# The last phase of an attention and mixture-of-experts kernel: half groups over seven PSUM banks, root scratch in the eighth, two additions on VectorE

## The chip, the cores and the metric

One core of a Trainium2 chip runs the whole program. The metric is the device time of one execution in microseconds (us); lower is better. The engines are named as in the profile: PE is TensorE's matmul side and PEld its weight loads, DVE is VectorE, ACT is ScalarE, POOL is GpSimd, SP is SyncE, whose queue issues most DMAs.

## The reference

A block of attention and a block of experts, each between layer norms, over 16 x 256 = 4096 tokens of width 256:

```
x = x + layernorm(attention(layernorm(x)))          # 16 heads of 128, weights = codes * scales
h = layernorm(x)
scores = softmax(h @ gate.T); keep 3 of 8 groups of experts, then 6 of 64 experts
slot of a token in an expert: its position, cut at 95 (CAPACITY 96: all later ones share slot 95)
out[e]  = (silu(buf[e] @ Wg[e].T) * (buf[e] @ Wu[e].T)) @ Wd[e].T
y       = sum over the 6 experts of weight * out[slot]
shared  = silu(h @ Sg.T) * (h @ Su.T) @ Sd.T
x = x + layernorm(y + shared)
```

The last line is what the change is about. All tokens past a capacity of 95 in an expert get the same output row, that of slot 95, weighted by their own weights.

## The kernel before

The program runs in three stages. Attention goes over 8 blocks of 512 tokens, then the 64 experts run one after the other (with the shared expert of the last blocks slipped between), and then comes the last phase, from about 1314 us to the end. Everything in it goes by groups of 512 tokens: NP = 8 groups, each held as 4 tiles of 128 tokens x 256. Every engine has its own instruction stream in program order, and waits on semaphores that others count up; nothing is scheduled at run time.

What the last phase does for a group g:

- SP loads two partial sums, `Y[0]` and `Y[1]`, from DRAM into `fin[g][:, 0]` and `fin[g][:, 1]` (two DMAs of 512 KB a group, 16 in all, semaphore `fl`). The experts have added their rows there; for groups 0 to 5 `Y[0]` also holds the shared expert's part. For groups 6 and 7 (`g >= LATE`) the shared part stays in SBUF, in `YL[g]`.
- POOL adds the two halves of `fin` (`last_sum`, L960, two instructions of 128x512 a group, semaphore `fa`).
- PE builds the sum in PSUM: `last_over` multiplies the transposed weights of the tokens past capacity, `W95T` (64 partitions), with the 64 rows `OUT95` (L1198); for groups 6 and 7 it adds `YL` by a matmul with the identity (L1203); `last_add` adds the sum from `fin` by a matmul with the identity (L1209, semaphore `fp`). One fp32 matmul stands in the profile as two instructions. `LB_` gives each group a pair of PSUM banks, four pairs in turn, so group g+4 must wait until ACT has read group g (semaphore `fn`).
- DVE takes mean and variance out of PSUM (`last_stats`: L1474 and L1478), and finds one over the square root for a batch of groups by a magic constant and three Newton steps: twelve small instructions on 128x8 or 128x4 numbers in SBUF, each of which waits for the one before (L1481 to L1487, the helper `step`; semaphore `fs`). `BATCH` says which groups share such a root: (0, 1), (2, 3), (4, 5), (6), (7).
- ACT normalizes from PSUM into `fin[g][:, 0]` with these scales and biases (L1355, four instructions a group).
- The residual `x1[g]` is added, the first half of the group by POOL (L970, semaphore `fx`) and the second by DVE (L1495, `fy`), and SP stores the group.

`POOL_LAST` is POOL's order: "s0 s1 s2 s3 x0 s4 x1 s5 x2 x3 s6 s7 x4 x5 x6 x7", with s for a sum and x for a residual. DVE does the statistics and root of a batch, and then the residuals of the batch before it. PE does the overs of groups 0 to 3, then the additions, and from group 4 on each over just ahead of its addition.

Of the kernel before, what the change touches and what calls it, by code (L numbers as in the profile page):

```python
# [18 lines left out]
E = 64  # L19
# [7 lines left out]
BATCH = ((0, 1), (2, 3), (4, 5), (6,), (7,))  # L27
POOL_LAST = "s0 s1 s2 s3 x0 s4 x1 s5 x2 x3 s6 s7 x4 x5 x6 x7"
EPS = 1e-5
# [5 lines left out]
LATE = 6  # L35
# [148 lines left out]
def build(nc, x, wc, wsc, wo_c, wo_s, bqkv, bo, gateT, sguT, sdT, ewT, ewd, out):  # L184
    ctx = ExitStack()
    with ctx:
# [36 lines left out]
        ident = sb("ident", [128, 128])  # L223
# [87 lines left out]
        def flat(a, dims):  # L311
# [20 lines left out]
                 "lf lc xr fo hd bi yi dd lb sw swh swl sg ssl saf sah sal sdn sy et ebt eg esl eac eo eow wix wt wtc fa fp fd fs fn fx fy").split()  # L332
# [455 lines left out]
        def _(eng):  # L788
# [99 lines left out]
            for g in range(NP):  # L888
# [3 lines left out]
            for g in range(NP):  # L892
                eng.wait_ge(s["fx"], g + 1)
                eng.wait_ge(s["fy"], g + 1)
                eng.dma_start(out[g * 512:(g + 1) * 512, :].rearrange("(t p) d -> p t d", p=128), fin[g][:, 0, :, :]
                              ).then_inc(s["fo"], 16)
# [4 lines left out]
        def _(eng):  # L901
# [54 lines left out]
            def last_sum(g):  # L956
                f = fin[g]
                eng.wait_ge(s_fl[g], 32)
                for h in range(2):
                    r = eng.tensor_tensor(half(f[:, 0], h), half(f[:, 0], h), half(f[:, 1], h), ALU.add)  # L960
                r.then_inc(s["fa"], 1)

            def last_x1(g):
                f = fin[g]
                eng.wait_ge(s["fn"], 2 * g + 1)
# [4 lines left out]
                eng.tensor_tensor(half(f[:, 0], 0), half(f[:, 0], 0), half(x1[g], 0), ALU.add).then_inc(s["fx"], 1)  # L970

            for name in POOL_LAST.split():
                (last_sum if name[0] == "s" else last_x1)(int(name[1:]))
# [3 lines left out]
        def _(eng):  # L977
# [212 lines left out]
            eng.wait_ge(s["wtc"], NP)  # L1190
            for k in range(4):
                eng.wait_ge(s_o95[k], 16 * E // 4)

            def last_over(g):
                if g >= 4:
                    eng.wait_ge(s["fn"], 2 * (g - 4) + 2)
                for t in range(4):
                    eng.matmul(LB_[g % 4][t // 2][:, t % 2 * 256:(t % 2 + 1) * 256],  # L1198
                               W95T[:, (4 * g + t) * 128:(4 * g + t + 1) * 128], OUT95[0:E, :],
                               start=(t % 2 == 0), stop=False, skip_group_check=True)  # L1200
                if g >= LATE:
                    for t in range(4):
                        eng.matmul(LB_[g % 4][t // 2][:, t % 2 * 256:(t % 2 + 1) * 256], ident[:, :],  # L1203
                                   YL[g][:, t, :], start=False, stop=False, skip_group_check=True)

            def last_add(g):
                eng.wait_ge(s["fa"], g + 1)
                for t in range(4):
                    r = eng.matmul(LB_[g % 4][t // 2][:, t % 2 * 256:(t % 2 + 1) * 256], ident[:, :],  # L1209
                                   fin[g][:, 0, t, :], start=False, stop=(t % 2 == 1), skip_group_check=True)  # L1210
                r.then_inc(s["fp"], 1)

            for g in range(4):
                last_over(g)
            for g in range(NP):
                if g >= 4:
                    last_over(g)
                last_add(g)
# [3 lines left out]
        def _(eng):  # L1222
# [127 lines left out]
            for g in range(NP):  # L1350
                eng.wait_ge(s["fs"], batch_of(g) + 1)
                for h in range(2):
                    for t in (2 * h, 2 * h + 1):
                        c = 4 * g + t
                        r = eng.activation(fin[g][:, 0, t, :], LB_[g % 4][h][:, t % 2 * 256:(t % 2 + 1) * 256],  # L1355
                                           ACT.Identity, bias=fNW[:, 3, c:c + 1], scale=fNW[:, 1, c:c + 1])
                    r.then_inc(s["fn"], 1)
# [3 lines left out]
        def _(eng):  # L1361
# [108 lines left out]
            def last_stats(gs):  # L1470
                for g in gs:
                    eng.wait_ge(s["fp"], g + 1)
                    for t in range(4):
                        r = eng.bn_stats(fST[g][:, t, :], LB_[g % 4][t // 2][:, t % 2 * 256:(t % 2 + 1) * 256])  # L1474
                step(r)
                c0, c1 = 4 * gs[0], 4 * gs[-1] + 4
# [10 lines left out]
                eng.scalar_tensor_tensor(out=b, in0=fMV[:, c0:c1, 0], scalar=-1.0, in1=y, op0=ALU.mult, op1=ALU.mult  # L1487
                                         ).then_inc(s["fs"], 1)

            def last_x1(g):  # L1490
                f = fin[g]
                eng.wait_ge(s["fn"], 2 * g + 2)
                if g < 4:
                    eng.wait_ge(s["xr"], 64)
                eng.tensor_tensor(half(f[:, 0], 1), half(f[:, 0], 1), half(x1[g], 1), ALU.add).then_inc(s["fy"], 1)  # L1495

            for n, gs in enumerate(BATCH):
                last_stats(gs)
                if n:
                    for g in BATCH[n - 1]:  # L1500
                        last_x1(g)
            for g in BATCH[-1]:
                last_x1(g)
# [35 lines left out]
```

## Time and profile before

| | us |
|---|---|
| median of 3 runs | 1377.25 (1375.5 to 1378.28) |
| the profiled execution | 1383.52 |
| its span in the trace | 1381.8 |
| last phase: first over to DVE's last instruction | 1316.6 to 1375.7 |
| PE busy over the span | 1223.8 (89%) |
| DVE, ACT, POOL busy over the span | 869.4, 826.4, 922.2 |

The profiled execution lies 1.7 us above its own span and 6.3 us above the median of the runs. Shares over the span say nothing of the last phase, which is a twentieth of it and has other limits than the rest.

### The profile page before, as it was taken

The page shows a single profiled execution, that of the slowest core. Times are in us where ns is not written, and L with a number is a line of the kernel's source. Part 1 is how long each engine was busy: PE and PEld are TensorE (multiplying, and loading weights), DVE is VectorE, ACT ScalarE, POOL GpSimd, SP SyncE. Part 2 cuts the span into 40 slices and gives each one's busy share as a digit, 9 for nine tenths or more (in the row PEclk, how much of TensorE's full clock was granted, in tenths as well). Part 3 has the DMA queues.
Part 4 walks back from the last instruction along what each step waited for, and adds up shares of the span by engine and source line. Part 5 has one row for each costly group of instructions (what it writes and reads, how often), then busy time and mean ns, then how long its engine had stood idle before and what let it go on. Part 6 is the DMA issues. An engine that isn't in the chain of part 4 may idle for free.

```text
span 1381.8 us, 25355 instructions
## 1 busy us (share of the span) xinstructions
PE 1223.8 (89%) x7876; PEld 855.4 (62%) x7876; DVE 869.4 (63%) x2285; ACT 826.4 (60%) x2128; POOL 922.2 (67%) x1126
## 2 busy tenths in 40 slices
PE   3789999999899999989999998998966998989984
PEld 1455666666566666666666666666634577768863
DVE  5766667677668758777976875777765333223337
ACT  2566668778677767777777677777733332223413
POOL 3576656568877877887887798688755523444554
PEclk9999999999999999999999999999977999999977
DMA  5556796755655444444535444444434569887683
GB/s 189 138 150 171 188 243 165 162 95 120 120 104 107 89 98 96 77 89 93 97 69 91 94 82 79 78 79 80 88 84 132 160 176 239 225 229 206 135 251 122
DMA packets 364678, 182.68 MB, mean 132 GB/s; under 512 B 287440, under 2 KB 343222, under 8 KB 364544
## 3 DMA queue, kind: packets, MB, share of 16 engines
q1 hardware_dynamic: 344960, 166.18, 50.8%
q0 software_dynamic: 16416, 11.70, 4.6%
q10 hardware_dynamic: 3168, 3.15, 0.7%
q8 instruction: 67, 1.10, 0.3%
q14 instruction: 67, 0.55, 0.1%
HBM read 75.32 MB, written 64.69 MB: 101 GB/s over the span
## 4 chain that ended last, share of the span: by engine, by line
PE 40%; DVE 20%; DMA 13%; POOL 12%; issue 7%; ACT 5%; SPq 2%; another core or an unknown queue 0%; ACTq 0%; POOLq 0%; DVEq 0%
PE bank L1029 7%; PE bank L1000 6%; PE bank L1044 6%; DMA PT<-PH 5%; DMA Y<-W,wix 5%; POOL P L931 4%; POOL PH L936 4%; PE bank L1015 4%; DVE nm L1397 3%; PE bank L1061 3%; PE bank L1163 3%; PE bank L1106 3%; PE bank L1176 2%; PE bank L1122 2%; POOL BUF L691 2%
## 5 line engine op out<-in xcount | busy, mean ns | idle before, releaser
L931 POOL TENSOR_SCALAR P<-P,rr 128x256 f32<-128x256 f32 x512 | 245.1, 491 | 148.1 <-DVE rr L1393 139.7
L1259 ACT ACTIVATE P<-bank,nm 128x256 f32<-128x256 f32 x512 | 237.6, 469 | 153.6 <-DVE nm L1397 143.3
L936 POOL TENSOR_TENSOR PH<-P,PH 128x512 f16<-128x512 f32 x256 | 297.7, 1178 | 16.3 <-ACT PH L1268 15.5
L1000 PE MATMUL bank<-RB,W 128*128 128x512 f16 x1092 | 261.0, 382 | 12.4 <-ACT Sx L620 4.1
L691 POOL DMA_INDIRECT BUF<-RT,ix x192 | 198.3, 1033 | 96.3 <-issue 40.9
L1029 PE MATMUL bank<-RB 128*128 128x256 f32 x1024 | 246.4, 384 | 2.9 <-ACT RB L1230 1.7
L1044 PE MATMUL bank<-PT,RB 128*128 128x256 f16 x1536 | 197.7, 274 | 29.8 <-DMA PT<-PH 26.5
L1397 DVE TENSOR_REDUCE nm<-bank 128x2 f32<-128x512 f32 x256 | 174.3, 681 | 53.8 <-PE bank L1029 53.3
L1029 PEld LDWEIGHTS bank<-RB 128*128 128x128 f32 x1024 | 186.4, 192 | 26.5 <-issue 2.7
L1044 PEld LDWEIGHTS bank<-PT,RB 128*128 128x128 f16 x1536 | 146.4, 98 | 88.0 <-DMA PT<-PH 41.5
L1268 ACT ACTIVATE PH<-P 128x512 f16<-128x512 f32 x256 | 161.3, 630 | 59.1 <-POOL P L931 45.7
L1000 PEld LDWEIGHTS bank<-RB,W 128*128 128x128 f16 x1092 | 106.4, 98 | 134.3 <-issue 18.0
L952 POOL DMA_INDIRECT Y<-W,wix x64 | 90.5, 1415 | 124.3 <-ACT W L1330 76.2
L1061 PE MATMUL bank<-W,O 128*128 128x256 f16 x1080 | 142.6, 276 | 30.3 <-DVE O L1403 26.8
L1061 PEld LDWEIGHTS bank<-W,O 128*128 128x128 f16 x1080 | 104.0, 99 | 79.2 <-DVE O L1403 25.9
L1377 DVE SCALAR_TENSOR_TENSOR RB<-bank,RB 128x512 f16<-128x512 f32 x128 | 87.9, 687 | 93.1 <-ACT RB L1237 85.7
L1015 PE MATMUL bank<-W,RB 128*128 128x512 f16 x550 | 140.5, 381 | 3.3 <-DVE RB L1377 3.3
L1259 ACT ACTIVATION_READ_ACCUMULATOR P<-bank,nm 128x1 f32 x512 | 101.1, 197 | 0.0
L1403 DVE SCALAR_TENSOR_TENSOR O<-bank,bqk,O 128x512 f16<-128x512 f32 x128 | 94.8, 740 | 3.6 <-issue 3.2
L1372 DVE TENSOR_SCALAR RB<-bank,bqk 128x512 f32<-128x512 f32 x128 | 95.4, 745 | 1.9 <-PE bank L1000 1.9
L1251 ACT ACTIVATE O<-bank,bqk 128x512 f16<-128x512 f32 x128 | 87.4, 683 | 14.6 <-PE bank L1044 8.4
L1230 ACT ACTIVATE RB<-bank,bqk 128x512 f32<-128x512 f32 x128 | 87.9, 687 | 3.0 <-PE bank L1000 3.0
(200 smaller groups left out, 1609.6 us busy)
## 6 DMA issues: line engine op xcount, KB each, us to landing
RB<-in_ewT SPq DMA_DIRECT2D x24, 352.0 KB
BUF<-zrow SPq DMA_DIRECT2D x4, 1926.0 KB, 8.6
W<-BUF SPq DMA_DIRECT2D x64, 120.4 KB
HT<-in_ewT SPq DMA_DIRECT2D x18, 352.0 KB
HT<-in_wc SPq DMA_DIRECT2D x24, 256.0 KB, 4.2
HT<-in_ws SPq DMA_DIRECT2D x24, 256.0 KB, 4.6
Y<-zrow SPq DMA_DIRECT2D x10, 512.0 KB, 3.2
RB<-in_ewd SPq DMA_DIRECT2D x24, 176.0 KB
```

What stands on the lines that cost most here:

```text
L691: eng.indirect_dma_start(BUF, bass.IndirectOffsetOnAxis(ap=ix[:, rt, t, k:k + 1], axis=0), RT[:, rt, t, :], None, bounds_check=CAP * E - 1 ...
L931: r = eng.tensor_scalar(p, p, rr[:, w % 4, t:t + 1], SP_, ALU.mult, ALU.mult)
L936: eng.tensor_tensor(PH[:, w % 2, 1, :], P[:, w % 2, :], PH[:, w % 2, 0, :], ALU.subtract).then_inc(s["pl"], 1)
L1000: r = eng.matmul(bk_[:, :], W[:, m, a, c * 2048 + h * 128:c * 2048 + (h + 1) * 128], XT[:, bp % 2, b, c, :], start=(k == 0), stop=(k == n ...
L1015: r = eng.matmul(bV[:, :], XT[:, bp % 2, a, c, t * 128:(t + 1) * 128], W[:, 2, b, c * 2048 + hg * 512:c * 2048 + (hg + 1) * 512], start=(k ...
L1029: r = eng.matmul(bS[u % 2][:, t * 256:(t + 1) * 256], QK[:, i % 2, 0, q * 256 + t * 128:q * 256 + (t + 1) * 128], QK[:, i % 2, 1, q * 256: ...
L1044: r = eng.matmul(bO[:, q * 256:(q + 1) * 256], V[:, i // 4 % 2, a, 2 * q + kc, h % 4 * 128:(h % 4 + 1) * 128], PT[:, u % 2, b, :, kc, :], ...
L1061: r = eng.matmul(bACC[q][:, t * 256:(t + 1) * 256], O[:, a, q * 256 + t * 128:q * 256 + (t + 1) * 128], W[:, 3, b, h * 256:(h + 1) * 256], ...
L1259: r = eng.activation(P[:, u % 2, t * 256:(t + 1) * 256], bS[u % 2][:, t * 256:(t + 1) * 256], ACT.Exp, bias=nm0[:, u % 4, t:t + 1], accum_ ...
L1268: eng.activation(PH[:, w % 2, 0, :], P[:, w % 2, :], ACT.Copy).then_inc(s["ph"], 1)
L1372: eng.tensor_scalar(QK[:, i % 2, 1, :], bP1[:, :], 1.0 / (SX * SW), bqk[:, 1, h:h + 1], ALU.mult, ALU.add).then_inc(s["kl"], 1)
L1397: eng.tensor_reduce(nm0[:, u % 4, :], bS[u % 2][:, :].rearrange("p (t k) -> p t k", t=2), AX, ALU.max, negate=True).then_inc(s["mx"], 1)
```

## The change

The last phase is cut into halves of groups, 16 pieces numbered i = 0 to 15, each 256 tokens and one PSUM bank. `GROUPS` puts groups 6 and 7 first, and `place(i)` gives the group and its half. `LB_` is now seven single banks used in turn, so piece i+7 waits for piece i to be read. The eighth bank, `bP0` (bank6), holds the means, the variances and the scratch of the roots, whose formula is regrouped so that most operands lie there; only `y` and the bias stay in SBUF. `BATCH` has six batches of 2, 3, 3, 3, 3 and 2 pieces. On PE the `YL` matmuls of the first four pieces come ahead of the wait for `OUT95`, then four overs (`AHEAD`), then sum and over in turn, the over four pieces ahead. Two pieces (`MIXED`: 13 and 15) are finished differently: ACT adds the bias to `x1` in SBUF, and DVE does scale and addition in one instruction out of PSUM (`last_mixed`). POOL adds the residual of the 14 others.

```diff
-BATCH = ((0, 1), (2, 3), (4, 5), (6,), (7,))
-POOL_LAST = "s0 s1 s2 s3 x0 s4 x1 s5 x2 x3 s6 s7 x4 x5 x6 x7"
+GROUPS = (6, 7, 0, 1, 2, 3, 4, 5)
+BATCH = ((0, 1), (2, 3, 4), (5, 6, 7), (8, 9, 10), (11, 12, 13), (14, 15))
+MIXED = (13, 15)
+PLAIN = [i for i in range(16) if i not in MIXED]
+AHEAD = 4
+POOL_LAST = ("s0 s1 s2 s3 s4 s5 s6 s7 x0 s8 x1 s9 x2 s10 x3 s11 x4 s12 x5 s13 x6 s14 x7 s15 "
+             "x8 x9 x10 x11 x12 x14").split()
+DVE_LAST = "b0 b1 b2 b3 b4 b5 v13 v15".split()
...
-        LB_ = ((bACC[0], bACC[1]), (bV, bO), (bS[0], bS[1]), (bP0, bP1))
+        LB_ = (bACC[0], bACC[1], bV, bO, bS[0], bS[1], bP1)
+        NL = len(LB_)
+        root = bP0[:, 0:64].rearrange("p (k t) -> p k t", k=2)
+        MV_ = bP0[:, 128:192].rearrange("p (t n) -> p t n", n=2)
...
+        def place(i):
+            return GROUPS[i // 2], i % 2
...
+            def last_part(i, part):
+                g, h = place(i)
+                if i >= NL and part != "sum" and (part == "yl" or g < LATE):
+                    if i - NL in MIXED:
+                        eng.wait_ge(s["fy"], MIXED.index(i - NL) + 1)
+                    else:
+                        eng.wait_ge(s["fn"], PLAIN.index(i - NL) + 1)
+                if part == "sum":
+                    eng.wait_ge(s["fa"], i + 1)
+                for t in range(2):
+                    n = 4 * g + 2 * h + t
+                    lhs, rhs = {"yl": lambda: (ident[:, :], YL[g][:, 2 * h + t, :]),
+                                "over": lambda: (W95T[:, n * 128:(n + 1) * 128], OUT95[0:E, :]),
+                                "sum": lambda: (ident[:, :], fin[g][:, 0, 2 * h + t, :])}[part]()
...
+            LATER = [i for i in range(2 * NP) if place(i)[0] >= LATE]
+            for i in LATER:
+                last_part(i, "yl")
             for k in range(4):
                 eng.wait_ge(s_o95[k], 16 * E // 4)
...
+            for i in range(AHEAD):
+                last_part(i, "over")
+            for i in range(2 * NP):
+                last_part(i, "sum")
+                if i + AHEAD < 2 * NP:
+                    last_part(i + AHEAD, "over")
...
+                for t in range(2):
+                    c, k = 2 * i + t, 2 * h + t
+                    if i in MIXED:
+                        r = eng.activation(x1[g][:, k, :], x1[g][:, k, :], ACT.Identity, bias=fNW[:, 3, c:c + 1])
+                    else:
+                        r = eng.activation(fin[g][:, 0, k, :], LB_[i % NL][:, t * 256:(t + 1) * 256],
                                            ACT.Identity, bias=fNW[:, 3, c:c + 1], scale=fNW[:, 1, c:c + 1])
-                    r.then_inc(s["fn"], 1)
+                r.then_inc(s["fb"] if i in MIXED else s["fn"], 1)
...
-                    r = eng.bn_aggr(fMV[:, c, :], fST[c // 4][:, c % 4, :])
+                    r = eng.bn_aggr(MV_[:, c, :], fST[c // 4][:, c % 4, :])
                 step(r)
-                v, y, a, b = (fNW[:, k, c0:c1] for k in range(4))
-                step(eng.tensor_scalar(v, fMV[:, c0:c1, 1], EPS, None, ALU.add))
+                v, b = (root[:, k, c0:c1] for k in range(2))
+                y, bias = fNW[:, 1, c0:c1], fNW[:, 3, c0:c1]
+                step(eng.tensor_scalar(v, MV_[:, c0:c1, 1], EPS, None, ALU.add))
                 step(eng.tensor_scalar(y.bitcast(I32), v.bitcast(I32), -0.5, RSQRT_MAGIC, ALU.mult, ALU.add))
                 for k in range(3):
-                    step(eng.tensor_tensor(a, y, y, ALU.mult))
-                    step(eng.scalar_tensor_tensor(out=b, in0=a, scalar=-0.5, in1=v, op0=ALU.mult, op1=ALU.mult))
+                    step(eng.tensor_tensor(b, v, y, ALU.mult))
+                    step(eng.scalar_tensor_tensor(out=b, in0=b, scalar=-0.5, in1=y, op0=ALU.mult, op1=ALU.mult))
                     step(eng.scalar_tensor_tensor(out=y, in0=b, scalar=1.5, in1=y, op0=ALU.add, op1=ALU.mult))
...
+            def last_mixed(i):
+                g, h = place(i)
+                eng.wait_ge(s["fb"], MIXED.index(i) + 1)
+                for t in range(2):
+                    c, k = 2 * i + t, 2 * h + t
+                    r = eng.scalar_tensor_tensor(out=fin[g][:, 0, k, :], in0=LB_[i % NL][:, t * 256:(t + 1) * 256],
+                                                 scalar=fNW[:, 1, c:c + 1], in1=x1[g][:, k, :],
+                                                 op0=ALU.mult, op1=ALU.add)
+                r.then_inc(s["fy"], 1)
+
+            for name in DVE_LAST:
+                (last_stats if name[0] == "b" else last_mixed)(int(name[1:]))
```

Two places of the program's order show it. The first is PE's queue in the middle of the last phase. Before, at group 4 (banks 4 and 5; `W` as input is the over, `ident` the addition): the over of four tiles waits for ACT (`s_fn`), then the addition waits for POOL (`s_fa`), and the over of group 5 follows.

```order
L1198 MATMUL bank4<-W 128x256 [waits s_fn]
L1198 MATMUL bank4<-W 128x256
L1198 MATMUL bank5<-W 128x256 x2
L1209 MATMUL bank4<-HT,ident 128x256 [waits s_fa]
L1209 MATMUL bank4<-HT,ident 128x256
L1209 MATMUL bank5<-HT,ident 128x256 x2
L1198 MATMUL bank2<-W 128x256 [waits s_fn]
```

Now, from the over of piece 9 (bank2) to that of piece 11 (bank0); the rows with `ident` are the sums of pieces 6 (bank7) and 7 (bank4).

```order
L1220 MATMUL bank2<-W 128x256 [waits s_fn]
L1220 MATMUL bank2<-W 128x256
L1220 MATMUL bank7<-RB,ident 128x256 [waits s_fa]
L1220 MATMUL bank7<-RB,ident 128x256
L1220 MATMUL bank3<-W 128x256 [waits s_fn]
L1220 MATMUL bank3<-W 128x256
L1220 MATMUL bank4<-RB,ident 128x256 [waits s_fa]
L1220 MATMUL bank4<-RB,ident 128x256
L1220 MATMUL bank0<-W 128x256 [waits s_fn]
```

Each sum of two tiles now stands behind an over that waits for the ACT pass of a piece seven earlier.

The second place is DVE at its second root. Before, batch (2, 3): eight statistics, then the root in `A` (SBUF) on 128x8.

```order
L1474 BN_STATS A<-bank0 128x6 [waits s_fp]
L1474 BN_STATS A<-bank0 128x6
L1474 BN_STATS A<-bank1 128x6 x2
L1474 BN_STATS A<-bank6 128x6 [waits s_fp]
L1474 BN_STATS A<-bank6 128x6
L1474 BN_STATS A<-bank7 128x6 x2
L1478 BN_AGGR A<-A 128x2 [waits s_fd]
L1478 BN_AGGR A<-A 128x2 x7
L1481 TENSOR_SCALAR A<-A 128x8 [waits s_fd]
L1482 TENSOR_SCALAR A<-A 128x8 [waits s_fd]
L1484 TENSOR_TENSOR A<-A 128x8 [waits s_fd]
L1485 SCALAR_TENSOR_TENSOR A<-A 128x8 [waits s_fd]
```

Now, batch (2, 3, 4): six statistics, each pair behind its own wait, then the root on 128x6 with bank6 among the operands.

```order
L1500 BN_STATS A<-bank2 128x6 [waits s_fp]
L1500 BN_STATS A<-bank2 128x6
L1500 BN_STATS A<-bank3 128x6 [waits s_fp]
L1500 BN_STATS A<-bank3 128x6
L1500 BN_STATS A<-bank0 128x6 [waits s_fp]
L1500 BN_STATS A<-bank0 128x6
L1504 BN_AGGR bank6<-A 128x2 [waits s_fd]
L1504 BN_AGGR bank6<-A 128x2 x5
L1508 TENSOR_SCALAR bank6<-bank6 128x6 [waits s_fd]
L1509 TENSOR_SCALAR A<-bank6 128x6 [waits s_fd]
L1511 TENSOR_TENSOR bank6<-bank6,A 128x6 [waits s_fd]
L1512 SCALAR_TENSOR_TENSOR bank6<-bank6,A 128x6 [waits s_fd]
```

No instruction of the root has two SBUF tensors as inputs any more, and the count of roots goes from five to six.

## Rows read from the trace of the kernel before

**Rows 1.** The page: its first line.

```profile
span 1381.8 us, 25355 instructions
```

**Rows 2.** Timeline of the last phase: start, length, engine, line, out<-in, count, idle before.

```profile
1312.74 1.07 PE L1176 MATMUL bank<-HT,W 88*96 88x256 f32 x4 [0.65 <-ACT W L1330]
...
1316.62 13.26 PE L1198 MATMUL bank<-W 64*128 64x256 f32 x32 [2.81 <-DMA W<-W]
...
1326.28 2.48 POOL L960 TENSOR_TENSOR RB<-RB 128x512 f32<-128x512 f32 x2 [7.71 <-DMA RB<-Y]
...
1329.81 7.72 PE L1209 MATMUL bank<-RB,ident 128*128 128x256 f32 x24
...
1335.84 1.42 DVE L1474 BATCH_NORM_STATS2 A<-bank 128x6 f32<-128x256 f32 x4 [0.79 <-PE bank L1209]
...
1337.30 0.64 DVE L1478 BATCH_NORM_AGGREGATE A<-A 128x2 f32<-128x6 f32 x8
...
1337.97 0.17 DVE L1481 TENSOR_SCALAR A<-A 128x8 f32<-128x8 f32 x1
...
1340.40 3.76 ACT L1355 ACTIVATE RB<-bank,A 128x256 f32<-128x256 f32 x8 [26.07 <-DVE A L1487]
...
1342.38 1.99 PE L1198 MATMUL bank<-W 64*128 64x256 f32 x8 [2.43 <-ACT RB L1355]
...
1367.36 1.28 DVE L1495 TENSOR_TENSOR HT<-HT,X 128x512 f32<-128x512 f32 x2
...
1374.76 0.94 DVE L1495 TENSOR_TENSOR W<-W,X 128x512 f32<-128x512 f32 x1 [1.40 <-ACT W L1355]
```

**Rows 3.** The same timeline: DVE's second and third roots beside POOL.

```profile
1340.28 2.74 DVE L1474 BATCH_NORM_STATS2 A<-bank 128x6 f32<-128x256 f32 x8
...
1341.49 1.26 POOL L970 TENSOR_TENSOR RB<-RB,SCf 128x512 f32<-128x512 f32 x1 [3.59 <-ACT RB L1355]
...
1343.73 0.28 DVE L1481 TENSOR_SCALAR A<-A 128x8 f32<-128x8 f32 x1
...
1345.16 1.26 POOL L970 TENSOR_TENSOR RB<-RB,SSf 128x512 f32<-128x512 f32 x1
...
1345.26 1.18 DVE L1484 TENSOR_TENSOR A<-A 128x8 f32<-128x8 f32 x1
...
1348.92 0.17 DVE L1484 TENSOR_TENSOR A<-A 128x8 f32<-128x8 f32 x1
...
1354.87 0.90 DVE L1481 TENSOR_SCALAR A<-A 128x8 f32<-128x8 f32 x1
...
1359.45 0.17 DVE L1486 SCALAR_TENSOR_TENSOR A<-A 128x8 f32<-128x8 f32 x1
```

**Rows 4.** Windows of PE: stretch, length, busy (count), granted clock, DMA share, GB/s.

```profile
1317.00:1317.50 0.50, 0.50 (x4) 0.88 0.26 16
...
1334.00:1334.50 0.50, 0.50 (x3) 0.55 1.11 348
...
1344.50:1345.00 0.50, 0.00 (x0) 0.69 1.12 354
...
1348.00:1348.50 0.50, 0.50 (x3) 0.90 0.00 0
```

**Rows 5.** The timeline again: PE's additions of group 4.

```profile
1345.25 3.38 PE L1209 MATMUL bank<-HT,ident 128*128 128x256 f32 x8 [0.88 <-POOL HT L960]
```

**Rows 6.** PE earlier, among the experts: timeline, then windows.

```profile
1238.18 4.44 PE L1106 MATMUL bank<-HT,W 128*96 128x512 f16 x12
...
1242.00:1242.50 0.50, 0.50 (x3) 0.72 0.88 237
```

**Rows 7.** Groups of DVE instructions over the span: busy, mean ns, idle before.

```profile
L679 DVE MAX8 c<-C 128x8 f32<-128x64 f32 x32 | 4.9, 215 | 0.3
...
L646 DVE TENSOR_TENSOR Tm<-Sx,gk 128x256 f32<-128x256 f32 x8 | 3.4, 429 | 0.3
...
L672 DVE SCALAR_TENSOR_TENSOR Sx<-bank,M 128x256 f32<-128x256 f32 x8 | 3.4, 424 | 0.3
```

More of the change, by code:

```diff
@@ L887, in _ @@
                 eng.wait_ge(s_ya[k], 16 * 32)
-            for g in range(NP):
+            for g in GROUPS:
                 for k in range(2):
@@ L891, in _ @@
                         "(t p) d -> p t d", p=128)).then_inc(s_fl[g], 16)
-            for g in range(NP):
-                eng.wait_ge(s["fx"], g + 1)
-                eng.wait_ge(s["fy"], g + 1)
+            for n, g in enumerate(GROUPS):
+                eng.wait_ge(s["fx"], sum(1 for i in PLAIN if i < 2 * n + 2))
+                if any(i < 2 * n + 2 for i in MIXED):
+                    eng.wait_ge(s["fy"], sum(1 for i in MIXED if i < 2 * n + 2))
                 eng.dma_start(out[g * 512:(g + 1) * 512, :].rearrange("(t p) d -> p t d", p=128), fin[g][:, 0, :, :]
@@ L954, in _, with last_sum, last_x1 @@
                                        compute_op=ALU.add).then_inc(s_ya[e % 2], 16)
-            def last_sum(g):
+            def last_sum(i):
+                g, h = place(i)
                 f = fin[g]
                 eng.wait_ge(s_fl[g], 32)
[L959 to L965, printed above, removed]
+                eng.tensor_tensor(half(f[:, 0], h), half(f[:, 0], h), half(f[:, 1], h), ALU.add
+                                  ).then_inc(s["fa"], 1)
+            def last_x1(i):
+                g, h = place(i)
+                f = half(fin[g][:, 0], h)
+                eng.wait_ge(s["fn"], PLAIN.index(i) + 1)
                 if g < 4:
@@ L969, in last_x1 @@
                     eng.wait_ge(s["po"], PO_END)
-                eng.tensor_tensor(half(f[:, 0], 0), half(f[:, 0], 0), half(x1[g], 0), ALU.add).then_inc(s["fx"], 1)
-            for name in POOL_LAST.split():
+                eng.tensor_tensor(f, f, half(x1[g], h), ALU.add).then_inc(s["fx"], 1)
+            for name in POOL_LAST:
                 (last_sum if name[0] == "s" else last_x1)(int(name[1:]))
@@ L1190, in _ @@
             eng.wait_ge(s["wtc"], NP)
+            def last_part(i, part):
+                g, h = place(i)
+                if i >= NL and part != "sum" and (part == "yl" or g < LATE):
[10 more added lines that the diff above has]
+                                "sum": lambda: (ident[:, :], fin[g][:, 0, 2 * h + t, :])}[part]()
+                    r = eng.matmul(LB_[i % NL][:, t * 256:(t + 1) * 256], lhs, rhs,
+                                   start=(t == 0 and (part == "yl" or part == "over" and g < LATE)),
+                                   stop=(t == 1 and part == "sum"), skip_group_check=True)
+                if part == "sum":
+                    r.then_inc(s["fp"], 1)
@@ L1191, in _ @@
+            LATER = [i for i in range(2 * NP) if place(i)[0] >= LATE]
+            for i in LATER:
+                last_part(i, "yl")
             for k in range(4):
                 eng.wait_ge(s_o95[k], 16 * E // 4)
[L1194 to L1218, printed above, removed]
+            for i in range(AHEAD):
+                last_part(i, "over")
@@ L1468, in step, with last_stats @@
                 eng.wait_ge(s["fd"], fd[0])
[L1470 to L1474, printed above, removed]
+            def last_stats(n):
+                for i in BATCH[n]:
+                    eng.wait_ge(s["fp"], i + 1)
+                    for t in range(2):
+                        r = eng.bn_stats(fST[i // 2][:, i % 2 * 2 + t, :], LB_[i % NL][:, t * 256:(t + 1) * 256])
@@ L1486, in last_stats @@
                     step(eng.scalar_tensor_tensor(out=y, in0=b, scalar=1.5, in1=y, op0=ALU.add, op1=ALU.mult))
-                eng.scalar_tensor_tensor(out=b, in0=fMV[:, c0:c1, 0], scalar=-1.0, in1=y, op0=ALU.mult, op1=ALU.mult
+                eng.scalar_tensor_tensor(out=bias, in0=MV_[:, c0:c1, 0], scalar=-1.0, in1=y, op0=ALU.mult, op1=ALU.mult
                                          ).then_inc(s["fs"], 1)
[L1490 to L1503, printed above, removed]
+            def last_mixed(i):
+                g, h = place(i)
+                eng.wait_ge(s["fb"], MIXED.index(i) + 1)
+                for t in range(2):
+                    c, k = 2 * i + t, 2 * h + t
[3 more added lines that the diff above has]
+                r.then_inc(s["fy"], 1)
```

22 lines of the change are left out of this document (12 added, 10 removed).

## The prediction, made before the changed kernel had run

> **What bounds the kernel now.** I read the page first, for the span [rows 1], then the chain that ended last, which in the last phase runs through PE to 1335.8 us and from there only through DVE, and then the timeline and the windows of that phase. The profiled execution took 1383.52 us, its span is 1381.8, and the median of the runs is 1377.25, so I work inside the span and carry the difference over. DVE's last instruction ends at 1374.76 + 0.94 = 1375.70 us [rows 2]; the 6.1 us from there to the span's end are one store of 512 KB and the closing of the program, the same in both kernels.
>
> The phase has two parts. To 1326.28 everything waits for the loads of Y [rows 2], and PE has time for the overs. The 16 loads are issued in the same number and sizes after the change, so POOL starts at the same time. From 1335.84 DVE is never idle: statistics, root, additions. A root of twelve dependent instructions lasts from 1337.97 to 1340.40, 2.43 us or 0.20 each, when POOL does nothing [rows 2]. When POOL works beside it, single instructions last 1.18 us, as long as POOL's addition of 1.26 us does [rows 3]. From 1343.73 to 1348.92 are five instructions, 5.2 us in place of 1.0; from 1354.87 to 1359.45 four, 4.6 in place of 0.8. These two holds cost 4.2 + 3.8 = 8.0 us on the chain. The statistics read PSUM, and eight of them took 2.74 us, 0.34 each, although a POOL addition began in the middle [rows 3].
>
> **The clock matters as much.** PE is at 2.4 GHz until 1317.4, having been idle up to 1316.6, and then at 1.2 until 1334.45; it falls again at 1344.7, after a pause, and rises at 1348.1 [rows 4]. One fp32 matmul of 256 columns costs 1.99 / 4 = 0.50 us at the upper level [rows 2]; the first 16 took 13.26 us, 0.76 of it at the upper level (1.5 matmuls), so 12.5 / 14.5 = 0.86 at the lower [rows 2, 4]. During all the overs, which use 64 partitions, PE was full and the clock stayed low for 12 us; it rose 4.6 us after the 128-partition additions had begun at 1329.81 [rows 2, 4], and in the second case 2.9 us after they began at 1345.25 [rows 4, 5].
>
> **The change, term by term.** I call a matmul pair of one piece a step: 1.0 us at the upper level, 1.73 at the lower.
>
> *What it removes.* The holds, 8.0 us, if a root whose operands lie mostly in PSUM isn't held: the PSUM-reading statistics were not [rows 3]. DVE's eight additions, 1.28 / 2 = 0.64 each [rows 2], 5.1 us. *What it adds to DVE.* A sixth root, 2.43, and four mixed instructions; a PSUM-and-SBUF instruction of 256 took 0.42 [rows 7], so 0.85 a piece and 1.7 in all. By DVE's work alone the sum is -8.0 - 5.1 + 2.4 + 1.7 = -9.0 us. But that only counts if DVE stays the bound, and I think it doesn't.
>
> *Scratch in PSUM.* No row shows DVE writing PSUM. Reading it costs nothing: 256 elements from a bank 424 ns, from SBUF 429 [rows 7]. The bounds are then 0 and, by the dearest small uncontested instruction, 0.215 us [rows 7] less 0.17, about 0.05 for each of some 60 instructions on the path, 3 us. No gain is seen in either row. I take 0. The Trainium skill speaks against the edit here: "VectorE: DVE Perf Modes", Specifications, says that VectorE sits closer to SBUF. By that each small instruction would be dearer, up to the 3 us just named; the two 256-element rows show no such difference.
>
> *The front.* The eight YL matmuls begin at 1312.74 + 1.07 = 1313.8 [rows 2], while the kernel before waited for OUT95; with eight over matmuls behind them PE is done at 1313.8 + 16 x 0.5 = 1321.8. Nothing waits for that. The first half-sum is there at 1326.28 + 2.48 / 2 = 1327.5 [rows 2]. So PE now pauses for almost 6 us, twice the 2.8 before which the clock fell, and I expect piece 0 to start at 1.2 GHz.
>
> *Up to piece 4.* Sum 0, over 4: 1327.5 + 2 x 1.73 = 1331.0. If the clock rises 4.6 us after the first sum, as before, at 1332.1, sum 1 ends at 1332.5. The root of pieces 0 and 1: statistics 0.69, four aggregates of 0.08 (0.64 / 8 [rows 2]), root 2.43, ACT for one piece 3.76 / 4 = 0.94 [rows 2], hand-overs 0.1: 1337.0. Over 7 waits for it. Then over 7 and sum 4: 1339.0.
>
> *The loop that I expect to bound.* Over i+7 waits for ACT's pass of piece i. The batch of pieces 2 to 4 can be rooted only after sum 4, while PE's queue holds over 9, which needs piece 2, ahead of sum 6. So each batch of three goes: last sum, statistics 0.69, six aggregates 0.48, root 2.43, ACT 0.94, hand-overs 0.15 = 4.7 us, in which PE has little to do (over 8, sum 5); then over, sum, over, sum = 4.0 us. 8.7 us for three pieces is 2.9 a piece. POOL brings them faster, one in 1.24 us once its loads are in. Before, DVE took 2.74 + 0.64 + 2.43 + 4.2 + 1.28 = 11.3 us for four pieces, the hold and two additions included [rows 2, 3], 2.8 a piece. So seven banks with batches of three give back what the free roots gain. Sum 4 to sum 7 and sum 7 to sum 10: 17.4; then 4.7 and five steps (over 15, sums 12 to 15): 9.7. Sum 15 ends at 1339.0 + 27.1 = 1366.1.
>
> *Clock in the loop.* PE works 4 of 8.7 us there. Before, with 1.99 us of over steps and a pause on either side, it fell at 1344.7 and came back after 3.4 us [rows 2, 4]. I allow two such falls; each makes 3.4 us of PE work cost 1 - 0.50 / 0.86 more, 1.4 us: +2.9, sum 15 at 1369.0.
>
> *The end.* Batch 4 is rooted 0.69 + 0.48 + 2.43 = 3.6 us after sum 13, that is 1.6 after sum 15; batch 5 needs 1.37 + 0.32 + 2.43 = 4.1 more; ACT then does pieces 14 and 15, 2.0; the mixed piece 15 0.85. POOL's x14 ends sooner (0.94 + 1.24). Together 8.6: 1377.6 us. The mixed pieces and POOL's 30 instructions (37 us from 1327 to 1377) are hidden; if POOL were late, x14 would be the next in line, 0.6 us behind the mixed piece at most.
>
> The sum: 1377.6 - 1375.7 = +1.9 us, and 1377.25 + 1.9 = **1379.2 us**. Its own range is 1376.5 to 1382.5: below with one fall less, above with the 3 us of PSUM.
>
> **The rivals.**
>
> *A. The forecast*, 0.40. For it: every duration has a row, and pieces 2, 3, 4 visibly share a root while over 9 waits.
>
> *B. The clock stays low.* Sums and overs in turn are half 64-partition work, a mixture that the trace doesn't have: full overs never raised the clock, full additions did [rows 2, 4], and so did 128x96 matmuls from 1238.18, at 1242.3 [rows 6]. If it never rises before the last four sums: nine steps to sum 4, 1327.5 + 15.6 = 1343.1; batches of 4.7 + 4 x 1.73 = 11.6, two of them, then 4.7 + 5 x 1.73 = 13.3: sum 15 at 1379.6. The end is 7.1 (batch 4's root is nearly done by then): 1386.7, so 1388.2 us. It decides if the clock is still at 1.2 by 1340. Chance 0.27.
>
> *C. The clock is up from the first sum and stays.* Then sum 1 is at 1330.5, the root at 1335.0, sum 4 at 1337.0, and 27.1 + 8.6 more: 1372.7, -3.0, 1374.2 us. For it: PE fell only twice in this phase before. Against it: the 6 us pause. Half-way cases, an early rise and no fall, lie between C and A. Chance 0.20.
>
> *D. DVE's saving comes through*, because hand-overs overlap better than I string them: -9.0 us, 1368.2 us. It needs PE to be ahead when over 9 is due, and the order of the queue forbids that. 0.08.
>
> *E. The roots are still held beside POOL*, or PSUM writes cost far more. Three roots lie in POOL's busiest stretch, at about 4 us each as in rows 3: +12 on C, +14 on A, about 1389 to 1393 us. 0.05. The Trainium skill, "SBUF — State Buffer", Who interferes with whom, says that a VectorE instruction with two SBUF inputs is held by a GpSimd one that reads SBUF, and one with at most one is not; by that page E is out.
>
> **The numbers.** 0.2% is 2.75 us, about what a measurement of this kernel can tell from no change: below 1374.5 is faster, above 1380.0 slower. Faster: D, most of C and a little of A, 0.27. Within: 0.24 of A and the rest of C, 0.27. Slower: 0.14 of A, B, E, 0.46. The range 1372 to 1389 takes in A, B and C and leaves out D and most of E.
>
> **What would show it.** Right: POOL's first sum at the old 1326.3; DVE's small root instructions at 0.17 beside a POOL addition; gaps on DVE of some 2 us a batch, ended by PE; PE waiting for ACT before the overs of pieces 9, 12 and 15; PE's clock at half when sum 0 starts. Wrong: DVE busy without a gap from 1330 (D), small instructions above 0.25 (scratch in PSUM costs), PE full at half clock past 1340 (B), or no wait of PE for ACT.

## The result, and the profile after

| | before | changed |
|---|---|---|
| median, us | 1377.76 (1375.50 to 1384.11, four runs) | 1397.26 (1394.60 to 1398.96, four runs) |
| ratio | | 1.0114, 95% interval 1.0076 to 1.0152 |
| profiled execution, us | 1383.52 | 1398.82 |

The change makes the kernel slower: the medians lie 19.5 us apart, and the ratio on record, which isn't the quotient of these two medians (that is 1.0142), stands for 15.7 us (10.5 to 20.9). The forecast was 1379.2 us with a range up to 1389: the range doesn't hold the result.

**The length of the last phase** is used below: from the start of POOL's first sum to the end of the last instruction of DVE or POOL. The start itself lay anywhere from 1315.7 to 1327.3 us in the profiled executions, although little ahead of it differs between the kernels. So a single time, and in part a median, carries some us that have nothing to do with the last phase. The runs were made in three sets besides this one, each with its own measurement of the kernel before (1377.11, 1380.65 and 1380.80 us); the ratios go by that, and medians of different sets compare only roughly. Before, the length was 1375.70 - 1326.28 = 49.4 us [rows 2].

The page of the changed kernel, its span and the clock in 40 slices (tenths of full speed). The last slices read 5: the clock was at its lower level through the last phase.

```profile
span 1397.1 us, 25367 instructions
...
PEclk9999999999999999999999999999888999999955
```

The timeline of the last phase (start, length, engine, line, out<-in, count, idle before and what ended it), which answers to [rows 2, 3]. `bank<-W,ident`, `RB,ident` and `HT,ident` are sums (128 partitions), `bank<-W` is an over (64 partitions).

```profile
1324.06 2.48 POOL L973 TENSOR_TENSOR W<-W 128x512 f32<-128x512 f32 x2 [7.61 <-DMA W<-Y]
...
1325.37 2.08 PE L1220 MATMUL bank<-W,ident 128*128 128x256 f32 x4 [5.94 <-POOL W L973]
1327.37 2.07 PE L1220 MATMUL bank<-W 64*128 64x256 f32 x4
...
1333.47 2.48 POOL L973 TENSOR_TENSOR RB<-RB 128x512 f32<-128x512 f32 x2 [0.91 <-DMA RB<-Y]
1333.51 0.16 DVE L1513 SCALAR_TENSOR_TENSOR A<-bank,A 128x4 f32<-128x4 f32 x1
1333.70 0.17 DVE L1511 TENSOR_TENSOR bank<-bank,A 128x4 f32<-128x4 f32 x1
...
1343.50 0.76 DVE L1500 BATCH_NORM_STATS2 A<-bank 128x6 f32<-128x256 f32 x2 [3.25 <-PE bank L1220]
...
1348.37 2.07 PE L1220 MATMUL bank<-W 64*128 64x256 f32 x4 [0.89 <-ACT W L1381]
...
1361.34 2.07 PE L1220 MATMUL bank<-W 64*128 64x256 f32 x4 [0.89 <-ACT RB L1381]
...
1374.33 2.07 PE L1220 MATMUL bank<-W 64*128 64x256 f32 x4 [0.90 <-ACT RB L1381]
1376.33 5.90 PE L1220 MATMUL bank<-HT,ident 128*128 128x256 f32 x16
...
1389.94 0.87 DVE L1522 SCALAR_TENSOR_TENSOR HT<-bank,A,X 128x256 f32<-128x256 f32 x2 [1.10 <-ACT X L1379]
```

Three things are to be seen. The steps on PE start 2.00 us apart, whatever their kind. DVE waits over 3 us for PE, then runs a root whose instructions take 0.17 us. And the overs at 1348.37, 1361.34 and 1374.33, those of pieces 9, 12 and 15, wait for ACT: every 13 us. The last instruction ends at 1390.81, so the phase has 66.8 us, 17.4 more than before. Here a step is the work of PE on one piece of one kind, a sum or an over, as in the prediction.

Windows of PE in the changed kernel (stretch, length, busy with count, granted clock, DMA share, GB/s), which answer to [rows 4]: 58 us at 0.50 of full speed, and the upper level only in the last steps, where sums follow sums.

```profile
1323.00:1381.00 58.00, 52.95 (x108) 0.50 0.54 173
1348.37:1361.34 12.97, 12.08 (x24) 0.50 0.12 40
...
1376.00:1380.50 4.50, 4.50 (x11) 0.50 0.35 117
1380.50:1382.30 1.80, 1.73 (x8) 0.92 0.00 0
```

In 12.97 us PE works 12.08: this is no pause in which a clock falls, but a full PE at half the clock. DVE is not the bound any more; its statistics' waits in the changed kernel (total us, times, longest):

```profile
DVE A L1500 <- PE bank L1220: 47.9, 14, 17.0
```

### The profile page after: what moved, and what is told of

Its sections match the earlier page's. It is cut to its first block, busy times and chain, and to the rows that moved or that the text cites. A ratio compares the mean times of both kernels' runs of the same rounds, so it can differ in the third digit from the quotient of the medians.

```text
span 1397.1 us, 25367 instructions
## 1 busy us (share of the span) xinstructions
PE 1239.6 (89%) x7876; PEld 860.1 (62%) x7876; DVE 857.4 (61%) x2293; ACT 826.6 (59%) x2128; POOL 929.2 (67%) x1132
## 4 chain that ended last, share of the span: by engine, by line
PE 44%; DVE 17%; DMA 12%; POOL 12%; issue 7%; ACT 5%; SPq 2%; another core or an unknown queue 1%; ACTq 0%; POOLq 0%; DVEq 0%
PE bank L1043 7%; PE bank L1014 7%; PE bank L1058 6%; DMA Y<-W,wix 5%; DMA PT<-PH 5%; POOL P L944 4%; POOL PH L949 4%; PE bank L1029 4%; PE bank L1075 4%; PE bank L1177 3%; PE bank L1120 3%; DVE nm L1423 3%; PE bank L1220 3%; POOL BUF L697 3%; PE bank L1190 2%
## 5 line engine op out<-in xcount | busy, mean ns | idle before, releaser
L1423 DVE TENSOR_REDUCE nm<-bank 128x2 f32<-128x512 f32 x256 | 174.3, 681 | 51.3 <-PE bank L1043 50.9
```

Of the source, the lines that this page charges most:

```text
L1423: eng.tensor_reduce(nm0[:, u % 4, :], bS[u % 2][:, :].rearrange("p (t k) -> p t k", t=2), AX, ALU.max, negate=True).then_inc(s["mx"], 1)
```

## The experiments

The theory after the result, T1: sums and overs in turn are half 64-partition matmuls, and that keeps the clock low. The rival T2: the 6 us pause ahead of the first sum lets the clock fall, and afterwards it doesn't rise because of the waits. The expectations call them theory 1 and theory 2; theory 3 is that the hand-over loop bounds whatever the clock. Below that lie the questions on which the prediction had a price: the hand-over loop, the roots' scratch, the mixed pieces.

**a_over128: the overs on 128 partitions.** Changed kernel; rows 64 to 127 of `OUT95` are zeroed once before the experts, so the added partitions add nothing to the sums.

```diff
-"over": lambda: (W95T[:, n * 128:(n + 1) * 128], OUT95[0:E, :]),
+"over": lambda: (W95T_all[:, n * 128:(n + 1) * 128], OUT95_all[:, :]),
...
+            eng.wait_ge(s["wo"], NU)
+            eng.memset(OUT95_all[64:128, :], 0.0).then_inc(s["oz"], 1)
```

> The changed kernel, but every over runs on 128 partitions: rows 64 to 127 of OUT95 are set to zero once, so the result is the same. Theory 1 (the clock stays at 1.2 GHz because half of the PE work in the last phase uses 64 partitions): the clock rises within about 7 us of the first sum, and the run is some 10 to 16 us faster than the changed kernel, 1381 to 1387 us. Theory 2 (the clock is down because of the pause before the first sum and the waits in the loop, whatever the partitions): no change, 1394 to 1399 us. Theory 3 (the hand-over loop bounds, the clock matters little): the clock rises but the gain is under 4 us.

Measured: 1382.19 us, ratio to before 1.0034 (1.0015 to 1.0053), phase 53.3 us: 13.4 less than in the changed kernel, by the partition count alone. Timeline and windows of a_over128:

```profile
1323.34 2.47 POOL L975 TENSOR_TENSOR W<-W 128x512 f32<-128x512 f32 x2 [7.75 <-DMA W<-Y]
1324.65 2.08 PE L1222 MATMUL bank<-W,ident 128*128 128x256 f32 x4 [6.55 <-POOL W L975]
1328.14 1.03 PE L1222 MATMUL bank<-W,ident 128*128 128x256 f32 x4
1329.01 1.03 PE L1222 MATMUL bank<-W 128*128 128x256 f32 x4
...
1340.80 1.23 PE L1222 MATMUL bank<-W 128*128 128x256 f32 x4 [3.17 <-ACT W L1384]
1341.83 1.91 PE L1222 MATMUL bank<-RB,ident 128*128 128x256 f32 x4
1343.53 1.81 PE L1222 MATMUL bank<-W 128*128 128x256 f32 x4
...
1351.11 1.30 PE L1222 MATMUL bank<-W 128*128 128x256 f32 x4 [3.17 <-ACT RB L1384]
...
1375.80 0.88 DVE L1528 SCALAR_TENSOR_TENSOR HT<-bank,A,X 128x256 f32<-128x256 f32 x2 [1.10 <-ACT X L1382]
```

```profile
1318.00:1328.00 10.00, 3.44 (x9) 0.66 0.95 303
1328.00:1340.00 12.00, 8.35 (x38) 1.00 1.10 350
1340.00:1345.00 5.00, 4.20 (x12) 0.67 1.04 338
```

PE stops even longer ahead of the first sum (6.55 us) and starts at the lower level too, and the clock is up 3.5 us after the first sum. This speaks for T1 and against the first half of T2. A step takes 0.87 us (1328.14 to 1329.01), and at the lower level 1.70 (1341.83 to 1343.53), not 2.00. What is left is the loop of the prediction: PE waits 3.17 us for ACT and goes round in 1351.11 - 1340.80 = 10.3 us for three pieces.

**b_warm: the pause filled in part.** Changed kernel, with ten matmuls whose result is thrown away ahead of the first sum.

```diff
             for i in range(AHEAD):
                 last_part(i, "over")
+            for _ in range(10):
+                eng.matmul(LB_[AHEAD][:, 0:256], ident[:, :], YL[LATE][:, 0, :], start=True, stop=True)
```

> The changed kernel with ten identity matmuls of 128 partitions added on PE after the first four overs, into a bank that is not yet in use; their result is thrown away. They fill the pause before the first sum. Theory 1 (64-partition overs between the sums keep the clock down): the first sums run at 2.4 GHz; if overs and sums in turn can't hold the clock, it falls within 10 us, gain under 5 us; if they hold it, though they can't raise it, the gain is 10 to 18 us. Theory 2 (the pause alone is to blame): the clock stays up, gain 12 us or more, 1379 to 1386 us.

Measured: 1390.55 us, 1.0107 (1.0065 to 1.0149), phase 66.1. Its timeline, then a window of PE in b_warm:

```profile
1319.48 1.41 PE L1220 MATMUL bank<-W,ident 128*128 128x256 f32 x4 [4.02 <-POOL W L973]
1320.82 2.07 PE L1220 MATMUL bank<-W 64*128 64x256 f32 x4
1322.82 2.07 PE L1220 MATMUL bank<-W,ident 128*128 128x256 f32 x4
```

```profile
1320.00:1320.50 0.50, 0.50 (x3) 0.70 1.11 346
```

The ten matmuls don't fill the pause: PE still stops for 4.02 us. The first sum starts at the upper level (1.41 us), the clock falls 0.7 us into it, before any over has followed, and every step after it is 2.00 us apart. In the kernel before, it fell in the same way 0.8 us after a stop of 2.81 us [rows 2, 4]. So the stop that is left can be the cause of this fall, and whether sums and overs in turn would lose an upper level that they have isn't shown. What b_warm shows is small: the state at the start makes 0.7 us in the phase.

**c_before_over128: the same edit on the kernel before**, `last_over` with all 128 partitions.

> The kernel before, with overs on 128 partitions and zeros below as in the first run of this set. Theory 1: the clock rises during the overs, about 4 to 7 us after they begin and not at their end, and does not fall at 1344.7; the first additions are done 3 to 4 us sooner, but DVE's chain of statistics and held roots bounds from there: 3 to 5 us faster than before. If partitions don't matter to the clock: no change.

Measured: 1379.32 us, 1.0016 (0.9992 to 1.0041), phase 49.1 against 49.4. The gain that was expected isn't there. Timeline of c_before_over128:

```profile
1317.73 8.83 PE L1200 MATMUL bank<-W 128*128 128x256 f32 x32 [2.89 <-DMA W<-W]
...
1337.78 1.18 DVE L1488 TENSOR_SCALAR A<-A 128x8 int32<-128x8 int32 x1
```

The first 16 overs took 8.83 us and not 13.26 [rows 2], so the clock does answer to the partitions in this kernel too. DVE comes to the end of its second group's statistics 2.0 us sooner after POOL's first sum. But its first root, which ran free in the kernel before, now lies beside a POOL sum and is held: two of its instructions take 0.79 and 1.18 us, 1.6 more than before. From there DVE's chain sets the end, and all but 0.4 us of the 2.0 is gone.

**d_roots_sbuf: the roots back in SBUF.** Changed kernel, otherwise as it is.

```diff
-        MV_ = bP0[:, 128:192].rearrange("p (t n) -> p t n", n=2)
+        MV_ = fMV
-                v, b = (root[:, k, c0:c1] for k in range(2))
+                v, b = (fNW[:, k, c0:c1] for k in (0, 2))
```

> The changed kernel with the roots' scratch, means and variances back in SBUF, the rest as changed. If PE's low clock is the bound, the holds of DVE beside POOL still sit in the loop of each batch: 1 to 3 us for each of some four batches, so 4 to 12 us slower than the changed kernel. If nothing on DVE is on the path: no change.

Measured: 1393.64 us, 1.0123 (1.0085 to 1.0161), phase 67.7, 1.0 more than the changed kernel. That is far less than expected. Timeline of d_roots_sbuf, POOL behind a root of the loop, and an instruction of the last root:

```profile
1355.53 1.26 POOL L983 TENSOR_TENSOR RB<-RB,SCf 128x512 f32<-128x512 f32 x1 [5.58 <-ACT RB L1380]
...
1380.11 1.19 DVE L1508 TENSOR_SCALAR A<-A 128x4 int32<-128x4 int32 x1
```

The four roots of this slow loop are not held at all, 0.17 us an instruction: POOL has run dry by the time that one starts (idle for the 5.58 us up to 1355.53, while a root runs from 1352.02), so there is nothing beside which it could be held. The first root and the last are held, by two instructions each. Only the last is on the way to the end, and its 1.5 us are the likely source of the 1.0.

**e_ahead2: the over two pieces ahead of the sum, not four.** Then the over of piece 9 stands behind sum 7, and the batch 5, 6, 7 no longer needs ACT's pass of piece 2 to be complete.

```diff
-AHEAD = 4
+AHEAD = 2
```

> The changed kernel with AHEAD 2 in place of 4: each over stands two pieces ahead of its sum, so that fewer sums queue behind an over that waits for ACT. Theory 1 (PE at 1.2 GHz, 2.0 us a step for 56 tiles or 28 steps, is the bound): no gain, last phase 66 to 68 us from POOL's first sum to DVE's last instruction, as in the changed kernel (66.8). Theory 3 (the loop of hand-overs bounds whatever the clock): 5 us or more faster.

Measured: 1399.46 us, 1.0142 (1.0097 to 1.0187), phase 67.6. No gain, though PE doesn't wait once: the first and the last of its 28 steps in turn, and the sums behind them, on the timeline of e_ahead2, then a window of PE over all 28:

```profile
1319.83 2.08 PE L1220 MATMUL bank<-W,ident 128*128 128x256 f32 x4 [7.52 <-POOL W L973]
...
1373.92 2.07 PE L1220 MATMUL bank<-W 64*128 64x256 f32 x4
1375.92 3.78 PE L1220 MATMUL bank<-HT,ident 128*128 128x256 f32 x8
```

```profile
1319.83:1375.92 56.09, 56.09 (x112) 0.50 0.51 163
```

(1375.92 - 1319.83) / 28 = 2.00 us a step. PE works 56.09 of 56.09 us and the clock is at its lower level throughout. That speaks against the second half of T2: without a single wait it doesn't rise either. With a_over128, T2 is out. Three waits of 0.9 us are gone, and two overs that had been done in the pause ahead of the first sum now stand behind it, 4.0 us. At this clock PE's own work sets the length.

**f_over128_ahead2: a_over128 and e_ahead2 together.**

> Overs on 128 partitions and AHEAD 2 together. With the clock up, the loop should be what is left: with AHEAD 4 PE waited 3.2 us for ACT before the overs of pieces 9, 12 and 15. If so, the last phase goes from 53 us to some 39 to 42, and the run to 1366 to 1370 us, faster than the kernel before. If the clock alone was the matter, AHEAD does nothing: 1380 to 1384 us.

Measured: 1372.22 us, 0.9934 (0.9906 to 0.9963), phase 39.4: 13.9 less than a_over128, and 10.0 less than the kernel before. The timeline, then PE's windows of f_over128_ahead2:

```profile
1315.72 2.48 POOL L975 TENSOR_TENSOR W<-W 128x512 f32<-128x512 f32 x2 [7.71 <-DMA W<-Y]
...
1331.57 2.27 DVE L1506 BATCH_NORM_STATS2 A<-bank 128x6 f32<-128x256 f32 x6
1336.75 2.27 DVE L1506 BATCH_NORM_STATS2 A<-bank 128x6 f32<-128x256 f32 x6
...
1354.22 0.88 DVE L1528 SCALAR_TENSOR_TENSOR HT<-bank,A,X 128x256 f32<-128x256 f32 x2 [1.10 <-ACT X L1382]
```

```profile
1317.00:1322.50 5.50, 5.47 (x13) 0.50 1.10 349
1322.50:1349.00 26.50, 24.30 (x109) 1.00 0.79 255
```

Now DVE is the bound, without idle time between two batches: three pieces in 1336.75 - 1331.57 = 5.2 us. The clock rises at 1322.7 and stays up; PE's longest stop behind that is 1.31 us. From 1334 on POOL doesn't stop any more, and the last sums wait for it (0.15 to 1.31 us), so POOL is close behind DVE as a bound.

**g_roots_sbuf: f with the roots in SBUF**, by d's edit.

> The second run of this set with the roots' scratch back in SBUF. In the changed kernel this cost nothing, since DVE waited there anyway. Now DVE is on the path: if a small instruction with only SBUF operands is held by POOL's additions, 8 to 16 us slower than the second run; if the holds were hidden here too, no change.

Measured: 1388.06 us, 1.0057 (1.0031 to 1.0082), phase 55.8. Where DVE is the bound, the scratch in PSUM is worth 16.4 us in the phase and 15.8 in the median. Timeline of g_roots_sbuf:

```profile
1331.99 2.48 POOL L974 TENSOR_TENSOR RB<-RB 128x512 f32<-128x512 f32 x2 [0.80 <-DMA RB<-Y]
1332.05 1.22 DVE L1516 TENSOR_TENSOR A<-A 128x4 f32<-128x4 f32 x1
1333.31 1.19 DVE L1517 SCALAR_TENSOR_TENSOR A<-A 128x4 f32<-128x4 f32 x1
1334.53 0.16 DVE L1518 SCALAR_TENSOR_TENSOR A<-A 128x4 f32<-128x4 f32 x1
```

Two instructions are held for as long as POOL's two additions last; the next, behind them, takes 0.16.

**h_no_mixed: f with `MIXED = ()`**: POOL adds the residual of pieces 13 and 15 too.

> The second run of this set with no mixed pieces: ACT normalizes pieces 13 and 15 from PSUM too, and POOL adds their residuals. POOL does the last piece in 0.94 + 1.26 us behind the root, where ACT and DVE took 0.94 + 0.94 + 0.86; with POOL's additions of pieces 14 and 15 one behind the other I expect 1 to 3 us slower; within 1 us if POOL isn't late.

Measured: 1372.33 us, 0.994 (0.9911 to 0.9969), phase 41.6. The mixed pieces are worth 2.2 us in the phase and nothing that the medians show.

**i_two_by_two: the changed kernel with PE's order two sums, two overs.** The overs stay on 64 partitions and as many as before; the changes from one kind to the other are halved.

```diff
-            for i in range(2 * NP):
+            for i in range(0, 2 * NP, 2):
                 last_part(i, "sum")
-                if i + AHEAD < 2 * NP:
-                    last_part(i + AHEAD, "over")
+                last_part(i + 1, "sum")
+                for j in (i + AHEAD, i + AHEAD + 1):
+                    if j < 2 * NP:
+                        last_part(j, "over")
```

> The changed kernel (overs on 64 partitions, AHEAD 4) with PE's order changed to two sums, then two overs. In the changed kernel each step takes 2.00 us at 1.2 GHz, with 128-partition overs 1.70. If the 0.3 us are the price of going from 128 to 64 partitions and back, only every second step pays it: steps of 2.0 and 1.7 in turn, last phase some 4 us shorter than 66.8 us. If four sums' worth of full-width work in a row also raises the clock, it is 8 us or more shorter. If the 0.3 us belongs to every step that waits on a semaphore, nothing changes.

Measured: 1384.51 us, 1.003 (1.0005 to 1.0056), phase 49.3. Its timeline on PE, then a window of PE in i_two_by_two:

```profile
1323.01 3.68 PE L1220 MATMUL bank<-W,ident 128*128 128x256 f32 x8 [5.76 <-POOL W L973]
1326.62 1.99 PE L1220 MATMUL bank<-W 64*128 64x256 f32 x8
1328.54 1.99 PE L1220 MATMUL bank<-W,ident 128*128 128x256 f32 x8
...
1338.52 1.13 PE L1220 MATMUL bank<-W 64*128 64x256 f32 x4 [2.98 <-ACT W L1383]
```

```profile
1323.00:1326.50 3.50, 3.49 (x8) 0.51 1.10 348
```

The clock rises at 1326.5, at the end of the first two sums, before an over has followed. It then stays up with 64-partition overs in between, until it falls at 1340.1, 1.6 us after PE had started again from a stop of 2.98 us for ACT; the next rise, at 1343.5, comes just behind two sums again. So T1 is too wide as it stands: with half the work on 64 partitions the upper level can be reached and held, and it stayed away with the piece-by-piece order. The changed kernel has no two sums in a row before its last four, and there its clock rises as well. Two in a row aren't always enough: e_ahead2's last two ended at 1379.7, after 3.78 us, without a rise. The order alone gives back 17.4 us of the phase.

**j_over128_ahead2_warm: f with the pause filled**, 15 thrown-away matmuls as in b_warm, which leave a stop of 1.59 us.

> The fastest kernel so far (overs on 128 partitions, AHEAD 2) with 15 identity matmuls on PE in the pause before the first sum, into a bank not yet in use. The first sums then run at 2.4 GHz and the first root is done some 2 us sooner, but the loads of Y give POOL its pieces no sooner: last phase 38 to 40 us, within 1 us of the kernel without them (39.4). If the first slow steps were on the path to the end: 2 us or more shorter.

Measured: 1363.55 us, 0.9878 (0.9826 to 0.993, four runs), phase 39.7. PE's windows of j_over128_ahead2_warm:

```profile
1304.00:1317.00 13.00, 11.48 (x54) 1.00 0.59 158
1317.00:1350.00 33.00, 28.04 (x120) 1.00 0.81 263
```

The clock is at the upper level all the time, but the phase isn't shorter than f's 39.4. The median lies 8.7 us below f's, but the two come from different sets, j's from four runs on another chip, and f's profiled execution, its fastest, took 1363.21 us. The difference comes from ahead of the last phase or from the runs' spread, since the phase doesn't show it; it isn't a measured worth of the filled pause.

## Why the prediction was wrong

**The failing step is "If the clock rises 4.6 us after the first sum, as before".** That rise was taken from a stretch in which 12 sums' worth of matmuls stood in a row [rows 2, 4]. The change puts an over of 64 partitions between any two sums, and there the clock stayed low for 55 us, from 1325.4 to about 1380.8. This is rival B, which the prediction described, with the point that decides it, and gave 0.27; the forecast A had 0.40. a_over128 differs from the changed kernel in the overs' partitions alone and shows the rise; i_two_by_two differs in the order alone and shows it too. Both have the stop of about 6 us ahead of the first sum, so that isn't what keeps the clock low, and e_ahead2 has no wait at all and stays low. Whether the clock rises depended on what ran, and the rows of one mixture can't be lent to another.

**And B's price was too small: a step costs 2.00 us, not 1.73.** 1.73 is right for either kind by itself: the overs in a row gave it [rows 2, 4], and a_over128's steps of one partition count 1.70. (At the upper level such a step took 0.87, not the 1.0 of the prediction.) The four instructions of a step start 0.43 us apart, and the first of the next step comes 0.72 after the fourth, so about 0.3 us lie at each change from 64 partitions to 128 or back. At the upper level i_two_by_two, with half the changes, has 1328.54 - 1326.62 = 1.92 us for two steps, 0.19 more than two of 0.865. The Trainium skill, "TensorEngine Tiling (Array Packing)", Key Properties, says that a change of tiling mode drains TensorE. Where the extra time stands would agree with that, but no run here shows that it is a drain, or that 64 and 128 partitions are two modes in the page's sense. The prediction gave the change of kind no price at all. In figures:

| from POOL's first sum, us | A | B | measured |
|---|---|---|---|
| end of sum 4 | 12.7 | 16.8 | 19.4 |
| loop for three pieces | 8.7 | 11.6 | 13.0 |
| end of sum 15 | 42.7 | 53.3 | 58.2 |
| end of the phase | 51.3 | 60.4 | 66.8 |

Up to sum 4 the excess over B is 9 x 0.27 = 2.4 and 0.1 of a later start. The loop is 4.7 + 4 x 2.0 = 12.7 by the prediction's own form with the measured step, 1.4 more than B in each of two. From sum 10 to sum 15 the changed kernel took 0.5 us less than B, since the last four sums follow each other without a change and the clock rises in them. The last 1.5 is B's end: it took batch 4's root as nearly done when sum 15 ended, but that root ended at 1383.90, 1.7 us behind the 1382.23 of sum 15, as in forecast A, whose end of 8.6 us was measured.

**The loop itself was right.** The waits of PE for ACT before the overs of pieces 9, 12 and 15 are there in the changed kernel and in a_over128, whose phase of 53.3 us is what forecast A, 51.3, would have been. It had three falls of the clock where the prediction allowed two, 1.4 us by its price. f_over128_ahead2 opens the loop, and 13.9 us go. Both faults hide each other: with the loop alone opened (e_ahead2) nothing is won, with the clock alone mended (a_over128) the kernel is still no faster than before.

**The roots.** "I take 0" for scratch in PSUM was right: small instructions with operands in PSUM took 0.16 to 0.17 us, also beside a POOL addition, and rival E is out. The worth of the removed holds, 8.0 us in the kernel before, was wrong to carry over: it is 1.0 us where PE is the bound (d_roots_sbuf) and 16.4 where DVE is (g_roots_sbuf, whose six roots are each held, by 1.5 to 5.0 us). The 8.0 was also short: in the kernel before, one more instruction is held in the fourth root (1.26 us at 1364.01), 1.1 us. And "DVE is never idle" leaves out its wait of 1.40 us for ACT ahead of the last addition [rows 2]. Neither touches the step that failed. The Trainium skill, "SBUF — State Buffer", Who interferes with whom, says that an instruction with two SBUF inputs is held beside a GpSimd one that reads SBUF, and that one with at most one isn't, unless it runs in a 2-port mode, which `tensor_scalar` can. The prediction left out this last condition. The rows agree with the whole: instructions with two inputs in SBUF are held, those with one of them in PSUM aren't, and TENSOR_SCALAR was held for up to 0.90 us in [rows 3].

**Rival D**, -9.0 us by DVE's work, was given 0.08 because "the order of the queue forbids that". That was so. When the order and the partitions are mended it comes true: f's phase is 10.0 us shorter than before.

**C** had the clock up from the first sum and staying. In b_warm it was up when the first sum started, and it didn't stay.

## What to carry to other kernels

A change that reorders work on PE changes what the clock sees: price every term that contains a matmul at both levels of the clock, and look whether the mixture of shapes in the new order has a row at all. Where it hasn't, the lower level is a case with its own sum, not a tail. In this kernel the half-filled matmuls between full ones were better filled up with zeros (a_over128) or kept together in twos (i_two_by_two). And with several faults in one phase, each mended alone may show nothing: f_over128_ahead2 beats the kernel before by 0.66% (0.37 to 0.94) out of two edits of which one alone gave 13.4 us back on a kernel that had lost 17.4, and the other nothing.

## What was unexpected of the hardware

- Sums of 128 partitions and overs of 64 in turn kept PE at half the clock for 55 us while it was busy 93% of the loop (12.08 of 12.97 us), and in e_ahead2 for 56.09 us while it never stopped. With all the overs on 128 partitions the upper level came in 3.5 us (a_over128) or 5.7 us (f_over128_ahead2), and with two sums in a row in 3.5 us, before the first over (i_two_by_two). That the two mendings also remove the changes of kind, wholly or by half, fits both observations; whether the empty half of the array or the time lost at the changes holds the clock down wasn't told apart. The overs in a row in the kernel before, without any change of kind, stayed low for 12 us too [rows 4], and with 128 partitions the clock rose 3.7 us after they began (c_before_over128), which speaks for the former.
- The clock fell only 0.3 to 1.6 us after PE had started again from a stop of 2.8 to 4.0 us (before, a_over128, b_warm, c_before_over128, i_two_by_two), so the first work behind a stop can still run at the upper level. Not each such stop did it: after 3.21 us in c_before_over128 the clock stayed up.
- A change between 64 and 128 partitions costs about 0.3 us at the lower level and 0.19 at the upper, for fp32 matmuls of 256 columns.
- DVE writes small results to PSUM as fast as to SBUF: 0.17 against 0.16 us on 128x4.
- The start of the last phase varied by up to 11.5 us between profiled executions. What it is that varies ahead of it stays open.
